# A two-layer attention kernel: split-row stacks packed without padding and moved part by part, small loads on ScalarE's queue, late weights loaded inside the first attention

## The reference

```
x = x + attention0(layernorm(x), ctx)          # 16 heads of width 8, mask on the keys, softmax
x = x + experts(layernorm(x))                  # 8 experts, top 2 of a router, 128 -> 512 -> 128
x = x + attention1(layernorm(x), layernorm(ctx))   # 16 heads of width 64, rope on the keys, logits clipped
x = x + quantised_linear(layernorm(x))
```

## Time and profile before

| | before |
|---|---|
| median of 3 runs | 311.63 us (310.9 to 312.22) |
| span of the profiled execution | 311.8 us |
| TensorE busy | 256.9 us, 82% |
| VectorE busy | 214.6 us, 69% |
| ScalarE busy | 129.9 us, 42% |
| GpSimd busy | 127.2 us, 41% |
| moved by DMA | 22.75 MB, mean 73 GB/s |

### The profile page before, as it was taken

The page is one execution under the profiler, slowest core; times in us unless marked ns, Lnnn a source line. Parts: engine busy times, 40 slices in busy tenths (PEclk is TensorE's granted clock), DMA queues, the critical chain, the costliest instruction groups (busy, mean ns, idle before and its releaser), DMA issues.

```text
span 311.8 us, 4749 instructions
## 1 busy us (share of the span) xinstructions
PE 256.9 (82%) x1772; PEld 171.1 (55%) x1772; DVE 214.6 (69%) x402; ACT 129.9 (42%) x194; POOL 127.2 (41%) x125
## 2 busy tenths in 40 slices
PE   1574069909999998998999999996799999999842
PEld 0261023304333545886888879774566768877531
DVE  3896038907887251377776944489999998699773
ACT  1073004406666786253354334473553543363200
POOL 7593000000000000043332453087889999499810
PEclk9999559966999999999999999999999999999995
DMA  6546344491450200002815600005864000000001
GB/s 174 150 124 118 130 97 107 121 286 57 127 147 1 71 2 0 2 1 47 186 40 119 154 0 2 1 2 135 188 160 125 2 0 2 0 2 1 3 0 34
DMA packets 16109, 22.75 MB, mean 73 GB/s; under 512 B 3022, under 2 KB 8886, under 8 KB 15798
## 3 DMA queue, kind: packets, MB, share of 16 engines
q1 hardware_dynamic: 15942, 22.44, 28.2%
q10 hardware_dynamic: 144, 0.00, 0.0%
HBM read 12.45 MB, written 1.45 MB: 45 GB/s over the span
## 4 chain that ended last, share of the span: by engine, by line
PE 32%; POOL 31%; SPq 10%; DVE 8%; issue 8%; DMA 7%; ACT 2%; POOLq 1%; DVEq 0%; ACTq 0%
PE b L874 20%; POOL v L517 15%; PE st L874 11%; POOL ctxT L520 9%; SPq L385 5%; DMA k_scr<-reg_z 3%; DMA ctx_tok<-in_ctx 2%; DMA reg_q<-maxpart 2%; SPq L331 2%; POOL reg_p L509 2%; DVE nmax L699 2%; POOL rstd L456 2%; POOL reg_k L477 1%; SPq L359 1%; ACT reg_p L603 1%
## 5 line engine op out<-in xcount | busy, mean ns | idle before, releaser
L699 DVE TENSOR_REDUCE nmax<-b 128x1 f32<-128x512 f32 x64 | 41.6, 686 | 29.3 <-PE b L874 29.3
L517 POOL TENSOR_TENSOR v<-reg_p 128x512 f32<-128x512 f32 x32 | 45.1, 1409 | 18.8 <-DVE reg_p L836 15.2
L874 PE MATMUL b<-reg_p,v 128*9 128x256 f32 (+1 forms) x512 | 49.0, 380 | 1.1 <-ACT reg_z L577 1.1
L618 ACT ACTIVATE reg_p<-st 128x1024 f32<-128x1024 f32 x32 | 31.6, 1025 | 37.6 <-PE st L874 34.9
L589 ACT ACTIVATE reg_z<-st,b 128x256 f32<-128x256 f32 x64 | 27.9, 474 | 30.3 <-PE st L874 30.3
L571 ACT ACTIVATE reg_p<-st 128x1024 f32<-128x1024 f32 x32 | 32.1, 1023 | 18.0 <-PE st L874 17.0
L874 PE MATMUL b<-reg_k,reg_q 96*128 96x512 bf16 x64 | 25.0, 430 | 16.1 <-DMA reg_k<-m_scr 14.8
L874 PE MATMUL st<-qq,kst 128*128 128x256 f32 x256 | 34.7, 289 | 0.0
L874 PEld LDWEIGHTS st<-qq,kst 128*128 128x128 f32 x256 | 31.5, 190 | 5.4 <-issue 4.6
L874 PEld LDWEIGHTS b<-w,reg_z 128*128 128x128 f32 x256 | 30.9, 192 | 4.6 <-issue 3.8
L874 PEld LDWEIGHTS b<-reg_p,v 128*9 128x9 f32 (+1 forms) x512 | 22.7, 113 | 18.2 <-issue 5.1
(11 more groups left out here) (149 smaller groups left out, 348.4 us busy)
## 6 DMA issues: line engine op xcount, KB each, us to landing
kst<-reg_p SPq DMA_DIRECT2D x48, 128.0 KB, 2.3
reg_k<-k_scr SPq DMA_DIRECT2D x6, 384.0 KB
w<-in_w SPq DMA_DIRECT2D x1, 2048.0 KB, 11.1
kst<-reg_q SPq DMA_DIRECT2D x16, 128.0 KB, 2.3
reg_q<-q_scr SPq DMA_DIRECT2D x6, 192.0 KB
k_scr<-reg_z SPq DMA_DIRECT2D x2, 384.0 KB, 5.4
ctxT<-in_ctxT SPq DMA_DIRECT2D x1, 512.0 KB, 4.7
ctx_tok<-in_ctx SPq DMA_DIRECT2D x1, 512.0 KB, 7.7
```

What stands on the lines that cost most here:

```text
L517: link(nc.gpsimd.tensor_tensor(half_sums, p4[:, 0:2, :], p4[:, 2:4, :], ALU.add))
L618: nc.scalar.activation(prob[:, u % RING1, :], st2[u % 2][:, :], ACT.Exp, scale=DK1 ** -0.5).then_inc(st_exp, 1)
L699: nc.vector.tensor_reduce(nmax[:, q, i:i + 1], bank[4 + mx % 2], AX.X, ALU.max, negate=True).then_inc(mx_done, 1)
L874: return nc.tensor.matmul(o, l, r, start=start, stop=stop)
```

## The change

1. **Packing.** The mask rows stay at 72, the maxima rows move from 96 to 75, and matmuls contract only the rows in use: 75 for the maxima, 78 for the scores. The four memsets of padding go. Two transfers from ScalarE's queue write the rows of ones, for both batches, from a small tile of ones.
2. **Part by part.** Each of the three key parts is written to the scratch as soon as it is split (`k_scr` has a new layout, d, part, head, column). The read-back of keys takes 24 rows as (d, part), that of queries broadcasts inside d: outermost counts 24 and 8 in place of 24 and 3. The mask rows of both batches are moved ahead of the stacks and counted by a semaphore of their own.
3. **Who splits.** VectorE splits batch 0 before it takes the statistics of the context; GpSimd splits batch 1 (with `xb` as its scratch). ScalarE copies yT.
4. **Queues.** ctxT is loaded in two halves, behind l0w. ScalarE issues both mask loads, lncol, wv1, the rows of ones and the small loads before its first activation.
5. **Late weights.** ScalarE issues w1, w2, wk1 and the eight rope loads between its exponentials, at units 1, 6, 12 and 16 to 19. SyncE does not issue them any more.

```diff
-MAX_ROW = 96
+STACK = NPART * DK0
+MASK_ROW = NPART * STACK
+MAX_ROW = MASK_ROW + NPART
+ALL_ROWS = MAX_ROW + NPART
...
 # SyncE
             load(x[:, :, :], a["x"].rearrange("t p d -> p t d"), in_x)
-            load(ctxT[:, :], a["ctxT"], in_ctxT)
             load(l0w[:, :, :], a["l0w"].rearrange("n p d -> p n d"), in_w0)
-            load(mask16[:, :], a["mask"].rearrange("a (p n) -> (a p) n", p=16), in_mask)
-            load(maskb[:, :], a["mask"].broadcast_to([P, C]), in_mask)
+            load(ctxT[:, 0:S2], a["ctxT"][:, 0:S2], in_ctxT0)
+            load(ctxT[:, S2:2 * S2], a["ctxT"][:, S2:2 * S2], in_ctxT1)
             load(ctx_tok[:, :, :], a["ctx"].rearrange("t p d -> p t d"), in_ctx)
-            load(wv1, a["wv1"], in_wv)
-            for dst, name in ((bias0, "bias0"), (bias1, "bias1"), (bias2, "bias2"), (brow, "brow")):
-                load(dst[:, :], a[name].broadcast_to([P, dst.shape[1]]), in_small)
...
+            sp.wait_ge(mparts, 1)
+            sp.dma_start(m_scr.rearrange("j (p n) -> p j n", p=16), mpart[:, :, :]).then_inc(scr_m, 16)
...
+                for j in range(NPART):
+                    sp.wait_ge(done, j + 1)
+                    sp.dma_start(k_scr[b, :, j], kp[:, j, :]).then_inc(scr_k[b], 16)
                 if b == 0:
                     sp.wait_ge(scr_m, 16)
+                    for c in range(B):
+                        sp.dma_start(Ks[MASK_ROW:MASK_ROW + NPART, c, :, :],
+                                     m_scr[:, None, c * S2:(c + 1) * S2].broadcast_to([NPART, H, S2])).then_inc(mask_rows, 16)
+                sp.wait_ge(done, NPART + 1)
+                sp.dma_start(q_scr[b].rearrange("i p t -> p i t"), qp).then_inc(scr_q[b], 16)
+                sp.wait_ge(scr_k[b], 16 * NPART)
+                for i in range(NPART):
+                    sp.dma_start(Ks[i * STACK:(i + 1) * STACK, b, :, :].rearrange("p h t -> p (h t)"),
+                                 k_scr[b].rearrange("d j h t -> (d j) (h t)")).then_inc(stack[b], 16)
+                sp.wait_ge(scr_q[b], 16)
+                for i in range(NPART):
+                    sp.dma_start(Qs[i * STACK:(i + 1) * STACK, b, :, :].rearrange("p h t -> p (h t)"),
+                                 q_scr[b, i].rearrange("(d h) t -> d (h t)", h=H)[:, None, :]
+                                 .broadcast_to([DK0, NPART, H * S])).then_inc(stack[b], 16)
...
 # GpSimd
-            link(nc.gpsimd.memset(reg_q[64:128, 0:2048], ONE_ONE))
             power(TT)
-            nc.gpsimd.memset(reg_k[64:128, 0:4096], 0.0).then_inc(consts, 1)
-            power(CT, 0)
...
             link(nc.gpsimd.memset(v0[:, :, :, DK0:DK0 + 1], 1.0))
-            link(nc.gpsimd.memset(reg_q[64:128, 2048:4096], ONE_ONE))
-            nc.gpsimd.memset(reg_k[64:128, 4096:8192], 0.0).then_inc(consts, 1)
+            power(CT, 0)
+            pool.wait_ge(kf_sb, 2)
+            part(nc.gpsimd.tensor_copy(kparts1[:, 0, :], kf[:, S2:2 * S2]))
+            link(nc.gpsimd.tensor_tensor(xb_flat, kf[:, S2:2 * S2], kparts1[:, 0, :], ALU.subtract))
+            part(nc.gpsimd.tensor_copy(kparts1[:, 1, :], xb_flat))
+            part(nc.gpsimd.tensor_tensor(kparts1[:, 2, :], xb_flat, kparts1[:, 1, :], ALU.subtract))
+            pool.wait_ge(q0_f, 1)
...
 # ScalarE
+            load(maskb[:, :], a["mask"].broadcast_to([P, C]), in_maskb)
+            load(mask16[:, :], a["mask"].rearrange("a (p n) -> (a p) n", p=16), in_mask)
             load(lncol[:, :], a["lncol"], in_cols)
+            load(wv1, a["wv1"], in_wv)
+            act.wait_ge(ones_set, 1)
+            act.dma_start(Ks[MAX_ROW:ALL_ROWS, :, :, :].rearrange("j b h n -> j (b h) n"),
+                          onesb[:, None, :].broadcast_to([NPART, B * H, S2])).then_inc(in_ones, 16)
+            act.dma_start(Qs[MASK_ROW:MAX_ROW, :, :, :].rearrange("j b (g h) n -> j (b g) (h n)", h=2),
+                          onesb[:, None, :].broadcast_to([NPART, B * H // 2, S2])).then_inc(in_ones, 16)
+            for dst, name in ((bias0, "bias0"), (brow, "brow"), (bias1, "bias1"), (bias2, "bias2")):
+                load(dst[:, :], a[name].broadcast_to([P, dst.shape[1]]), in_small)
...
+            act.wait_ge(tr, 1)
+            nc.scalar.activation(yT[:, :], bank[7], ACT.Copy).then_inc(yT_sb, 1)
             act.wait_ge(q0_ps, 1)
             nc.scalar.activation(qf, bank[6], ACT.Copy, scale=1.0 / math.sqrt(DK0)).then_inc(q0_f, 1)
...
+                    if u == 1:
+                        load(w1[:, :, :], a["w1"].rearrange("e p f -> p e f"), in_w1)
+                    elif u == 6:
+                        load(w2[:, :, :, :], a["w2"].rearrange("e (f p) d -> p e f d", p=P), in_w2)
+                    elif u == 12:
+                        load(wk1[:, :, :], a["wk1"].rearrange("p (n c) -> p n c", n=2 * G), in_wk)
+                    elif 16 <= u < 20:
+                        load(cosT[32 * (u - 16):32 * (u - 15), :], a["cosT"], in_rope)
+                        load(sinT[32 * (u - 16):32 * (u - 15), :], a["sinT"], in_rope)
...
 # VectorE
             norm_apply(y, x, 0, TT)
+            dve.wait_ge(in_maskb, 16)
+            dve.wait_ge(k0_ps, 1)
+            nc.vector.tensor_tensor(kf[:, 0:S2], bank[4], maskb[:, 0:S2], ALU.mult).then_inc(kf_sb, 1)
+            dve.wait_ge(kf_sb, 1)
+            part(nc.vector.tensor_copy(kparts[:, 0, :], kf[:, 0:S2]))
...
+            dve.wait_ge(q0_f, 1)
...
             dve.wait_ge(in_ctx, 16)
             norm_stats(ctx_tok, 0, CT, at=0)
+            dve.wait_ge(k0_ps, 2)
+            nc.vector.tensor_tensor(kf[:, S2:2 * S2], bank[5], maskb[:, S2:2 * S2], ALU.mult).then_inc(kf_sb, 1)
+            dve.wait_ge(pow_done, 2)
...
 # TensorE
-                        pe.wait_ge(stack[b], 16 * 8)
+                            pe.wait_ge(kf_sb, 2)
+                            pe.wait_ge(mask_rows, 16 * B)
+                            pe.wait_ge(in_ones, 16 * 2)
+                        pe.wait_ge(stack[b], 16 * 2 * NPART)
```

More of the change, by code:

```diff
@@ L177, in build @@
                 b4[:, :], b5[:, :], b6[:, :], b7[:, :]]
-        in_x, in_w0, in_ctxT, in_mask, in_ctx, in_cols, in_wv, in_rope, in_wk, in_small, in_w1, in_w2, \
+        in_x, in_w0, in_ctxT0, in_ctxT1, in_mask, in_maskb, in_ctx, in_cols, in_wv, in_rope, in_wk, in_small, in_w1, in_w2, \
             in_wq, in_wo = (sem("in_" + n) for n in (
-                "x", "w0", "ctxT", "mask", "ctx", "cols", "wv", "rope", "wk", "small", "w1", "w2", "wq", "wo"))
+                "x", "w0", "ctxT0", "ctxT1", "mask", "maskb", "ctx", "cols", "wv", "rope", "wk", "small", "w1", "w2", "wq", "wo"))
         consts = sem("consts")
+        ones_set, in_ones = sem("ones_set"), sem("in_ones")
         pool_step = sem("pool_step")
@@ L191, in build @@
         q0_f, v0_sb = sem("q0_f"), sem("v0_sb")
-        parts = sem("parts")
+        kf_sb, parts, parts1 = sem("kf_sb"), sem("parts"), sem("parts1")
         mparts = sem("mparts")
-        scr_k, scr_q = sem("scr_k"), sem("scr_q")
-        scr_m = sem("scr_m")
+        scr_k, scr_q = [sem(f"scr_k{b}") for b in range(B)], [sem(f"scr_q{b}") for b in range(B)]
+        scr_m, mask_rows = sem("scr_m"), sem("mask_rows")
         stack = [sem(f"stack{b}") for b in range(B)]
@@ L363, in _ @@
[L363 to L379, removed]
-                sp.dma_start(Ks[MAX_ROW:MAX_ROW + NPART, b, :, :].rearrange("j h (k n) -> j (h k) n", n=P),
-                             onesb[:, None, :].broadcast_to([NPART, H * KT, P])).then_inc(stack[b], 16)
+                done = parts if b == 0 else parts1
@@ L391, in _ @@
-            load(wk1[:, :, :], a["wk1"].rearrange("p (n c) -> p n c", n=2 * G), in_wk)
+                    for c in range(B):
[4 more added lines that the diff above has]
+                sp.wait_ge(scr_k[b], 16 * NPART)
@@ L653, in layer_norm, with part @@
                 norm_apply(dst, src, first, tiles)
-            def split(dst, src, tmp):
-                link(nc.vector.tensor_copy(dst[0], src))
-                link(nc.vector.tensor_tensor(tmp, src, dst[0], ALU.subtract))
-                link(nc.vector.tensor_copy(dst[1], tmp))
-                return nc.vector.tensor_tensor(dst[2], tmp, dst[1], ALU.subtract)
+            done_parts = [0]
+            def part(ins):
+                done_parts[0] += 1
+                ins.then_inc(parts, 1)
+                dve.wait_ge(parts, done_parts[0])
             def take(item):
@@ L690, in _ @@
+            dve.wait_ge(k0_ps, 2)
+            nc.vector.tensor_tensor(kf[:, S2:2 * S2], bank[5], maskb[:, S2:2 * S2], ALU.mult).then_inc(kf_sb, 1)
+            dve.wait_ge(pow_done, 2)
+            nc.vector.scalar_tensor_tensor(out=shift[:, :], in0=mv[:, 0:CT, 0], scalar=-1.0, in1=rstd[:, 0:CT],
+                                           op0=ALU.mult, op1=ALU.mult).then_inc(ctx_shift, 1)
             nc.vector.memset(bank[6], 0.0).then_inc(o0_sb, 1)
```

95 lines of the change are left out of this document (34 added, 61 removed).

## The result

The changed kernel takes 296.9 us in the median of four runs (296.07 to 297.29); the kernel before beside it 311.56 (310.9 to 312.22). The ratio is 0.9527, interval 0.9508 to 0.9545: 14.7 us faster. The forecast was 295, range 288 to 302. The profiled execution took 296.07 us with a span of 294.3. The intervals here compare undisturbed executions only; where kernels scatter, the text gives the whole range.

What follows compares the result with a forecast made beforehand. Two queue waits that leave TensorE idle before the scores were taken as the bound at the start. Scores 17.1 us earlier plus 1.0 for the clock minus 1.7 given back is 16.4: 311.6 to 295.2, said as 295, range 288 to 302.

Steps and rivals of the forecast that it cites:

- two queue waits: SyncE's issues of mask rows, 7.65 and 9.03 us; TensorE idle 14.77 us before the maxima, 7.28 before the scores.
- the give-back: ScalarE's late-weight issues between exponentials: costs 1.7 us (0 if all hides, 5.5 if none does).
- Start of the maxima: First matmul of the maxima at 34.2 instead of 41.65, set by TensorE's chain through the context's values.
- the 0.5 allowed: Added to the start of the maxima for ScalarE's 14 issues, about 10 us, ahead of its first copy.
- signs of being wrong: Several-us issue on ScalarE's queue ahead of yT or between exponentials; maxima waiting for a stack; context normalised after 28.
- the stack: Batch 0's keys and queries land at 27 to 30, before 34.2, so hidden under TensorE's chain.
- From the maxima to the scores: 18.2 us from first maxima to first scores, which start at 52.4 against 69.5: 17.1 us earlier.
- the near tie: Before the scores: TensorE's maxima and values take 17.9 us, the first rows of maxima land after 18.3.
- Clock in the first scores: First four rounds of scores at full instead of half clock: another 1.0 us saved.
- (a): Rival: stack ends last, loads at 5.6, clock not fallen; maxima at about 29, time 290 us; chance 0.15.
- (c): Rival: ones transfers hold ScalarE's queue 7.65 to 9.0 us each before its first copy; 308 or 312 us; chance 0.04.
- (b): Rival: ScalarE's issues held by a full queue, or late loads hold the exponentials; 5 us, 300 us; chance 0.17.

Runs made afterwards that it cites:

- the second profiled execution: The changed kernel itself, unaltered, run again as the base for the experiments: 295.68 us (295.3 to 301.36), ratio 0.9467.
- the other profiled run of the same start: The kernel before with only rope, wk1, w1 and w2 moved from SyncE to ScalarE; maxima started at 40.48; 305.55 us, ratio 0.9793.
- two profiled executions (316.76 and 317.7 us): Changed kernel with late weights issued by SyncE again: all of them (median 309.18 us), then rope and wk1 alone (median 314.72 us).

## Why the prediction was right, step by step

The path was right: two queue waits ahead of TensorE went, and the times up to the scores came within 1.2 us. That the sum came out within 2 us is in part luck, because errors of both signs met in it. Between the two profiles 17.5 us were saved, where the sum had 16.4: 1.2 less from the start of the maxima, 0.6 more from the clock, 1.7 more from the give-back that didn't come. Between the medians it is 14.7. The profiled execution of before had a span of 311.8; the later executions of that kernel whose spans are known have 308.7 to 311.2, with times 1.8 above their spans. If that holds for it too, its time was 313.6, about 2 us above the median, and its span was not its whole time. The profiled execution of the changed kernel, 296.07, is 0.8 below its median. Subtracting a span's saving from the median of the runs left both out: 17.5 - 2.0 - 0.8 is the 14.7.

**Start of the maxima: 34.2 forecast, 35.43.** Of TensorE's chain the loads were put at 8.2 and came at 9.26. ScalarE's issues cost more than the 0.5 allowed: it was free at 12.81, then came the table load until 14.12, which the sum didn't have at all; so yT was copied 1.8 us after its turn at 12.33. One of the prediction's own signs of being wrong shows here, an issue of several us ahead of yT:

```profile
6.54 3.41 ACTq L513 DMA_DIRECT2D bias<-in_bias  x2
```

The second keys and the queries took 1.12 and 1.13 us instead of 2.07 each, which gave 1.9 back; that was chance, for in the second profiled execution the same keys took 2.08. The values ended at 34.8, 0.6 past the forecast, at half clock as foreseen.

**The step that was mis-sized is the stack: 27 to 30 forecast, 35.3 measured.** I took 180 GB/s from one window of before for the keys and let the queries follow. Keys and queries, 1728 KB, took from 18.65 to 35.3, 16.6 us, so 106 GB/s. But they were not alone. Part by part also means that batch 1's parts, 576 KB, are written to the scratch in the same stretch, from 24.21 on; in the kernel before these writes were issued at 34.12. The reading of the second stack, which waits for its keys' writes, is issued only at 37.11. With them the whole stretch moved 142 GB/s. Two windows of the changed kernel, between the issues:

```profile
24.00:26.00 2.00, 0.00 (x0) 0.00 (x0) 0.00 (x0) 2.00 (x7) 1.85 (x3) 0.50 0.65 115
...
30.00:32.00 2.00, 2.00 (x3) 0.67 (x2) 0.00 (x0) 0.57 (x1) 0.03 (x1) 0.50 0.57 107
```

```profile
24.21 2.65 SPq L349 DMA_DIRECT2D k_scr<-reg_z  x3
...
28.71 0.38 SPq L356 DMA_DIRECT2D q_scr<-reg_y  x1
...
37.11 1.11 SPq L359 DMA_DIRECT2D reg_k<-k_scr  x3
```

The stack was called hidden under the values; here it ended last, if by 0.6 us, which is the second of the prediction's signs of being wrong. It is a tie, though: of the five profiled executions in which the stack is moved as in the changed kernel and its start isn't shifted by an edit, the stack releases the maxima in one and the values do in four, at 35.0 to 36.1. So moving the stack's start earlier or the values alone earlier gains little. Its end is hardly moved by the splits: with keys issued at 17.7, 18.65, 20.05 and 20.56 the stack landed at 35.3, 35.3, 36.0 and 35.2. It is later with the outermost count of 3 (3.8 us) and with the ones just ahead of it (5.8 us in two runs). What holds it at 106 GB/s stays open; batch 1's writes beside it are the first suspect, and no run moved them alone.

The rule on how many engines a transfer uses (the Trainium skill, DMA: Bandwidth & Descriptors, section "Why a DMA increments its semaphore by 16 and not by 1") was taken to change nothing in the sum. The run with outermost count 3 agrees with it, share 0.19, and shows that the row order changes 4 us.

**From the maxima to the scores: 18.2 forecast, 18.17.** Right, and the near tie held: 1 MB of other loads in the same queue turned it into a wait of 2.0 us.

**Clock in the first scores: 1.0 forecast, 1.6.** Right in kind.

**ScalarE's give-back: 1.7 forecast, nothing seen.** The copies that end a group of four units are 6.50 us apart over the rope loads where before they were 6.45 (78.45 to 84.95, and 96.00 to 102.45). I added issue time to activation time, but the rows overlap:

```profile
79.81 1.02 ACT L576 ACTIVATE reg_p<-st 128x1024 f32<-128x1024 f32 x1 [0.98 <-PE st L879]
79.89 0.35 ACTq L513 DMA_DIRECT2D reg_r<-in_cosT  x1
80.27 0.44 ACTq L513 DMA_DIRECT2D reg_r<-in_sinT  x1
80.76 1.02 ACT L576 ACTIVATE reg_p<-st 128x1024 f32<-128x1024 f32 x1
```

The next two loads are issued while the activation runs.

**Parts.** The late weights alone are worth 6.4 us on the kernel before. In the changed kernel the medians with these loads on ScalarE and on SyncE are 13.5 us apart, but the nearest execution only 2.6 (298.29 against 295.68). The profiled ones of the rest have a long stretch at half clock, whose cause isn't shown. The row order of the stack is worth about 4. The earlier start of the maxima, 6.2 us between the two profiles and about 5 against the other profiled run of the same start, comes from the stack's waits that went together with packing, part-by-part moving and the new queues; beyond the row order it wasn't taken apart. The part that loads small things on ScalarE's queue has a price: with the masks there x lands 3 us late, and yT waits for 14 issues. Removing the memsets made y 3 us shorter, but later loads took that back; the packing by itself wasn't run. Of the rivals, (a) came with its first half, the stack last, but with the loads late and the clock low; (c) didn't come; of (b) the hold of 3.41 us came, and cost little. No version's median was below the changed kernel's.

## What to carry to other kernels

A short wait on TensorE may cost more than itself: look at what the clock does behind it and at single executions, not the median alone. Two matmuls in the gap cost nothing here and are worth a try. A load is cheapest where nothing urgent shares its queue or its engines. Here transfers with an outermost count of 3 just ahead of the stack made it 5.8 us later. When a transfer is slower than its window promised, ask what else now moves beside it. Before a saving read from a span is taken off the median, the profiled execution must be placed among the runs.

## What the runs showed that I had not expected

- In two profiled executions (316.76 and 317.7 us), after 2.0 us of idle ahead of the scores and 2.5 us of work, the granted clock was at half for 48 us, with TensorE busy nearly all of them. In the kernel before, two longer stretches of idle were followed by only 6 us of low clock under work. Why the short one was followed by so long a fall, and only in some executions, stays open.
- The first matmuls run at half rate though the record grants full clock: 2.04 us at 9.26 and 1.12 at 13.43 for the same shape, both in windows of clock 1.00. The kernel before has 2.07 at 6.78 and still 2.08 at 14.97. In the second profiled execution of the changed kernel the one at 13.03 still took 2.08.
- Eight small loads issued by 41.9 had landed only at 52.8 (wf, 64 KB) beside the stack of batch 1.
